# Six local-attention layers: cycles of half a sequence, one TensorE loop body, inverse roots by guess and products

## The reference, cut to what matters

```python
x = attn_layer(shift_tokens(x), Wqkv[i], ...) + x     # 16 heads of 64, window 32, look back one window
x = ffn_layer(shift_tokens(x), ln_g[i], ...) + x      # layer norm, 128 -> 2x341, gelu gate, -> 128
# in attn_layer, for q and k: t / max(norm(t), 1e-12) * scale, then the rotary turn with tables for every token
```

## Time and profile before

| | us |
|---|---|
| median of 3 runs (lowest, highest) | 4182.8 (4181.38, 4186.91) |
| the profiled execution's own time | 4189.23 |
| its span in the trace | 4187.4 |
| PE busy | 3726.9 (89%) |
| DVE busy | 3097.7 (74%) |
| POOL busy | 2984.4 (71%) |
| ACT busy | 2239.1 (53%) |

### The profile page before, as it was taken

How to read it: one execution, slowest core, us unless ns; L and a number is a source line. 1 busy time by engine, 2 the same in 40 slices (tenths; PEclk the granted TensorE clock), 3 DMA queues, 4 the chain that set the end, 5 groups by cost and what they waited for, 6 DMA issues and landing times. The chain is left out here.

```text
span 4187.4 us, 157873 instructions
## 1 busy us (share of the span) xinstructions
PE 3726.9 (89%) x67688; PEld 2899.3 (69%) x67880; DVE 3097.7 (74%) x4664; ACT 2239.1 (53%) x2808; POOL 2984.4 (71%) x1330
## 2 busy tenths in 40 slices
PE   6888886899999899999999999999899998999995
PEld 4555554677777677777777777777777777777773
DVE  3455454778788788887787877787878788887883
ACT  3444443556565565555555655565555555555551
POOL 1100103888888788888888888888878888888882
PEclk9999997999999999999999999999999999999997
DMA  1000000222222322222322223222223222222221
GB/s 50 4 5 3 3 5 21 70 78 67 63 63 70 80 64 64 64 69 59 81 68 64 59 68 84 64 64 64 69 55 84 64 67 59 69 64 64 64 64 51
DMA packets 162242, 239.53 MB, mean 57 GB/s; under 512 B 42258, under 2 KB 60632, under 8 KB 161496
## 3 DMA queue, kind: packets, MB, share of 16 engines
q1 hardware_dynamic: 161624, 230.00, 21.3%
HBM read 21.00 MB, written 4.19 MB: 6 GB/s over the span
## 5 line engine op out<-in xcount | busy, mean ns | idle before, releaser
L1057 POOL TENSOR_TENSOR norms<-floors,minus_half 128x16 f32<-128x16 f32 x384 | 1127.9, 2937 | 212.4 <-DVE floors L1397 212.3
L1061 POOL TENSOR_TENSOR by_cos<-by_cos,by_sin 128x1024 f32<-128x1024 f32 x384 | 947.0, 2466 | 268.9 <-DVE by_sin L1390 266.4
L1067 POOL TENSOR_TENSOR by_cos<-by_cos,norms 128x1024 f32<-128x1024 f32 x384 | 734.2, 1912 | 29.5
L1290 ACT ACTIVATE squares<-proj 128x1024 f32<-128x1024 f32 x384 | 393.3, 1024 | 491.9 <-PE proj L1132 453.5
L1388 DVE TENSOR_TENSOR by_cos<-proj,turns 128x1024 f32<-128x1024 f32 x384 | 468.9, 1221 | 246.7 <-ACT squares L1290 200.8
L1130 PE MATMUL proj<-qkv_hi,xs_hib 128*128 128x512 f32 x1152 | 537.3, 466 | 41.8 <-DVE by_sin L1390 26.9
L1394 DVE TENSOR_REDUCE sumsb<-squares 128x16 f32<-128x1024 f32 x384 | 464.7, 1210 | 89.8 <-ACT squares L1290 89.8
L1132 PE MATMUL proj<-qkv_hi,xs_lob 128*128 128x512 f32 x1152 | 468.4, 407 | 0.0
L1131 PE MATMUL proj<-qkv_lo,xs_hib 128*128 128x512 f32 x1152 | 467.7, 406 | 0.0
L1390 DVE TENSOR_TENSOR by_sin<-proj,turns 128x1024 f32<-128x1024 f32 x384 | 466.0, 1214 | 0.0
L1139 PE MATMUL ring<-ident,by_cos 128*128 128x128 f32 x3072 | 408.9, 276 | 6.8 <-issue 5.8
(11 more groups left out here) (171 smaller groups left out, 7397.2 us busy)
## 6 DMA issues: line engine op xcount, KB each, us to landing
v_win<-vb SPq DMA_DIRECT2D x1152, 130.0 KB
v_win<-vb SPq DMA_DIRECT2D x768, 65.0 KB
in_qkv<-L_ffn_Wqkv SPq DMA_DIRECT2D x12, 768.0 KB
wo<-L_ffn_Wo SPq DMA_DIRECT2D x6, 512.0 KB, 4.1
x_tok<-L_attn_x SPq DMA_DIRECT2D x8, 256.0 KB, 4.6
residual<-x_tok SPq DMA_DIRECT2D x8, 256.0 KB, 2.0
o_x<-residual SPq DMA_DIRECT2D x1, 2048.0 KB, 7.9
out<-o_x SPq DMA_DIRECT2D x8, 256.0 KB, 2.3
```

Source lines behind the costliest of these rows:

```text
L1057: nc.gpsimd.tensor_tensor(norms[:, t % 2, j, :], floors[:, t % 2, j, :], c["minus_half"][:, 0:H], ALU.pow).then_inc(e[f"{w_}_norm"].sem, 1)
L1061: nc.gpsimd.tensor_tensor(by_cos[:, j, :], by_cos[:, j, :], by_sin[:, j, :], ALU.add).then_inc(e[f"{w_}_added"].sem, 1)
L1067: nc.gpsimd.tensor_tensor(heads, heads, norms[:, t % 2, j, :].unsqueeze(2).broadcast_to([P, H, DH]), ALU.mult).then_inc(e[f"{w_}_ready"].s ...
```

## The change

- A cycle is now half a sequence (two tiles, `PER = 2`), and the feed-forward part runs once for each half in 256 columns, two halves later (`LAG = 2`). `Events` give more credit (`ahead`).
- PE has one loop body for every half of a layer. What differed between cycles is moved off PE: the mask of a sequence's first window is copied by a DMA into `mask_now` once for each half, the wait for `Wo` is on ACT, the bias product of a new layer stands ahead of the loop. The other engines keep loops over sequences 2 to 6 with two halves in the body and write out four halves around each layer's end.
- kT holds two tiles as a ring, EK waits for the scores of the tile before. `by_cos` is doubled. C waits for the transposes of two tiles before and for A of the tile before.
- The power on POOL for the norms is replaced: ACT makes a guess for q and k together (IG, an Exp of the floor's bits read as an integer), and POOL refines it with two Newton rounds of four products of 128 x 32, each waiting for the one before. The floor for q and k is one DVE instruction.
- DG is gone; spread is two transposes for each half of f_rstd broadcast over 128 columns.
- A layer's w1 is scaled inside the ACT copy and the DVE subtraction, and one DVE instruction (L1447) goes.

```diff
 CYCLE = {
+    "PE": "Tq:0 mean Pq:2 X:-1 O:-2 V:-1 Tk:0 Pk:2 var S:0 spread Tk:1 Pv:2 Tq:1 W:-2 O:-1 Pq:3 X:0 W:-1 V:0 "
+    "Pk:3 GG AA S:1 Pv:3 F4",
+    "Act": "XF XSa:2 EV:1 EXP:-1 EQ:0 Qq:2 EX:-1 IG:1 EO:-2 XSa:3 FSQ EK:0 Qk:2 XH EK:1 EV:2 EQ:1 EXP:0 IG:2 "
+    "EO:-1 Qq:3 EX:0 Qk:3 GEL",
+    "DVE": "XSd:2 Rk:1 XC Rq:2 Cq:2 R:-1 FV Ck:2 XM MX:0 SB:0 XSd:3 Rk:2 XL WX:-2 Cq:3 WX:-1 Rq:3 R:0 Ck:3 AM "
+    "MX:1 SB:1 XN",
+    "Pool": "Aq:0 N:0 Mq:0 Ak:0 Mk:0 Aq:1 Ak:1 N:1 Mk:1 FP Mq:1",
+    "SP": "VM:0 VM:1",
 }
...
+            def inverse_roots(t, when):
+                x, y, z = floors[:, t % 2, :], norms[:, t % 2, :], newton[:, :]
+                wait_tile(pool, "guess", t, when)
+                for n, limit in enumerate((c["three"], c["twelve"])):
+                    if n:
+                        wait_tile(pool, "newton", t, when, 4)
+                    nc.gpsimd.tensor_tensor(z, y, y, ALU.mult).then_inc(e["newton"].sem, 1)
+                    wait_tile(pool, "newton", t, when, 4 * n + 1)
+                    nc.gpsimd.tensor_tensor(z, z, x, ALU.mult).then_inc(e["newton"].sem, 1)
+                    wait_tile(pool, "newton", t, when, 4 * n + 2)
+                    nc.gpsimd.tensor_tensor(z, limit[:, :], z, ALU.subtract).then_inc(e["newton"].sem, 1)
+                    wait_tile(pool, "newton", t, when, 4 * n + 3)
+                    nc.gpsimd.tensor_tensor(y, y, z, ALU.mult).then_inc(e["newton" if n == 0 else "norm"].sem, 1)
...
-                    nc.gpsimd.tensor_tensor(norms[:, t % 2, j, :], floors[:, t % 2, j, :], c["minus_half"][:, 0:H],
-                                            ALU.pow).then_inc(e[f"{w_}_norm"].sem, 1)
...
+                elif kind == "IG":
+                    wait_tile(act, "floor", t, when)
+                    for x in "qk":
+                        wait_tile(act, f"{x}_ready", t - 2, when)
+                    nc.scalar.activation(norms[:, t % 2, :], floors[:, t % 2, :].bitcast(I32), ACT.Exp, scale=GUESS_SCALE,
+                                         bias=c["guess_bias"][:, 0:1]).then_inc(e["guess"].sem, 1)
...
                 elif kind == "spread":
-                    wait_seq(pe, "diag", cyc)
+                    wait_half(pe, "f_rstd", when)
-                    nc.tensor.matmul(out[:, 0:S], ones[:, :], diag[:, :, :].rearrange("p t n -> p (t n)"), start=True,
-                                     stop=True).then_inc(e["spread_full"].sem, 1)
+                    for i in range(PER):
+                        last = nc.tensor.transpose(out[:, i * P:(i + 1) * P], f_rstd[:, i:i + 1].broadcast_to([P, P]),
+                                                   ident[:, :])
+                    last.then_inc(e["spread_full"].sem, 1)
...
+            for at in range(-LEAD, LAG):
+                cycle(at, None, at)
...
+            with pe.Fori(0, DEPTH - 1) as layer:
+                bias_of(layer, pe.snap(layer * STEPS + LAG))
+                with nc.Fori(LAG, STEPS + LAG, engines=one, hint_back_edge=True) as n:
+                    cycle(pe.snap(layer * STEPS + n), layer)
```

More of the change, by code:

```diff
@@ L759 @@
 PART = {"q": 0, "k": 1, "v": 2}
-CYCLE = {
[10 rows of a table removed]
-}
[L774 to L779, removed]
+HALVES = S // (2 * P)
+PER = TILES // HALVES
+HS = PER * P
+STEPS = B * HALVES
+LEAD = 2
+BIAS_SLOT = 0
+GUESS_SCALE = float(-0.5 * np.log(2.0) / 2 ** 23)
+GUESS_BIAS = float(0.5 * np.log(2.0) * (127 - 0.043))
+GUESS_ERROR = 3.33e-4
+ROOT_SCALE = 16.0
+LAG = 2
+CYCLE = {
+    "PE": "Tq:0 mean Pq:2 X:-1 O:-2 V:-1 Tk:0 Pk:2 var S:0 spread Tk:1 Pv:2 Tq:1 W:-2 O:-1 Pq:3 X:0 W:-1 V:0 "
[6 more added lines that the diff above has]
+    "SP": "VM:0 VM:1",
+}
+FFN = ("XF", "mean", "XC", "FSQ", "var", "FV", "FP", "spread", "XM", "XH", "XL", "GG", "GEL", "AA", "AM", "F4", "XN")
+RELEASE = {"Tq": ("q_T", 1), "Tk": ("k_T", 1), "X": ("pT", 1), "V": ("attn", 2), "O": ("oT", 1), "W": ("x_mid", 1),
+           "mean": ("centred", 1), "var": ("f_var", 1), "spread": ("xn", 1), "GG": ("gelu", FC), "AA": ("gated", FC),
+           "F4": ("x_new", 1)}
+RINGS = ("Tq", "Tk", "X", "V", "O", "W", "mean", "var", "spread", "GG", "AA", "F4")
 def tokens(engine):
@@ L803, in in_cycle, with steps_of @@
 def in_cycle(name, t):
-    return next(at for _, n, at in tokens("PE") if n == name and (at - t) % TILES == 0)
-def steps_of(engine, kind):
+    return next(at for _, n, at in tokens("PE") if n == name and (at - t) % PER == 0)
+def steps_of(engine, at=None, begin=0, end=None):
     steps = []
-    for token, name, t in tokens(engine):
[L813 to L835, removed]
@@ L963, in run, with wait_tile @@
[L963 to L968, removed]
-            def middle(layer):
[L971 to L975, removed]
+        def wait_tile(eng, name, t, when, k=1):
+            base, p = when
+            eng.wait_ge(e[name].sem, e[name].at((t + PER * p) * (e[name].per // PER) + k, base))
@@ new lines, in wait_half, with wait_moved, where, columns @@
+        def wait_half(eng, name, when, k=1):
+            base, p = when
+            eng.wait_ge(e[name].sem, e[name].at((p - LAG) * e[name].per + k, base))
+        def wait_moved(eng, t, when):
+            base, p = when
+            moved = e[f"v_moved{t % PER}"]
+            eng.wait_ge(moved.sem, moved.at((p + t // PER) * 160 + 160, base))
+        def where(b, p, t):
+            off, tile = divmod(PER * p + t, TILES)
+            return (off % B if b is None else b + off), tile
+        def columns(b, p, t, rows, begin, end):
+            seq, tile = where(b, p, t)
+            return xT[rows, bass.ds(seq, 1), 1 + tile * P + begin:1 + tile * P + end].rearrange("p a n -> p (a n)")
@@ new lines, in layers_stage, with run, cycle @@
+        low, high, every = slice(0, P // 2), slice(P // 2, P), slice(0, P)
+        def run(eng, name, step, new_layer=lambda layer: None):
+            def cycle(when, b, layer, *place):
+                for s_, t, token, ahead in steps_of(name, *place):
+                    step(s_, t, token, when, b, layer + ahead if ahead else layer)
+            def middle(layer):
+                with eng.Fori(LAG, B - 1) as b:
+                    base = eng.snap(layer * STEPS + b * HALVES)
+                    for p in range(HALVES):
+                        cycle((base, p), b, layer)
+            for at in range(-LEAD, HALVES * LAG):
+                cycle((0, at), None, 0, at)
@@ L976, in run @@
             with eng.Fori(0, DEPTH - 1) as layer:
-                cycle("second", layer * B + 1, 1, layer)
                 new_layer(layer)
                 middle(layer)
-                cycle("last", layer * B + (B - 1), B - 1, layer + 1)
-                cycle("first", layer * B + B, 0, layer + 1)
-            cycle("second", (DEPTH - 1) * B + 1, 1, DEPTH - 1)
+                base = eng.snap(layer * STEPS)
+                for at in range(STEPS - HALVES, STEPS + HALVES * LAG):
+                    cycle((base, at), None, layer, at)
@@ L983, in run @@
             middle(DEPTH - 1)
-            cycle("end", DEPTH * B - 1, B - 1)
-            cycle("tail", DEPTH * B, 0)
+            for at in range(STEPS - HALVES, STEPS + HALVES * LAG):
+                cycle(((DEPTH - 1) * STEPS, at), None, DEPTH - 1, at, 0, PER * STEPS)
         def all_loaded(new):
             return new * (16 * LOADS) + 16 * LOADS
-        def previous(b):
-            return B - 1 if isinstance(b, int) and b == 0 else b - 1
-        def following(b):
-            return 0 if isinstance(b, int) and b == B - 1 else b + 1
@@ L1033, in _ @@
             sp.wait_ge(padded, 2)
-            run(sp, "SP", step, new_layer=new_layer)
+            run(sp, "SP", step, new_layer)
             sp.wait_ge(loaded, DEPTH * 16 * LOADS)
@@ L1181, in step @@
                 elif kind == "O":
-                    wait_tile(pe, "attn", t, cyc, 2)
-                    out = take(SLOT[token], cyc, "oT", tile_at("oT", t, 1), new)
+                    wait_tile(pe, "attn", t, when, 2)
+                    out = take(token, kind, t, when, new)
                     for i in range(PAIRS):
@@ new lines, in ffn @@
+                    wait_half(pe, "f_rstd", when)
+                    out = take(token, kind, t, when, new)
+                    for i in range(PER):
+                        last = nc.tensor.transpose(out[:, i * P:(i + 1) * P], f_rstd[:, i:i + 1].broadcast_to([P, P]),
+                                                   ident[:, :])
+                    last.then_inc(e["spread_full"].sem, 1)
+                elif kind in ("GG", "AA"):
+                    part, full = (1, "gate_full") if kind == "GG" else (0, "up_full")
+                    wait_half(pe, "xn_lo", when)
+                    out = take(token, kind, t, when, new)
+                    for k in range(FC):
+                        cols, at = slice(k * P, (k + 1) * P), slice(k * HS, (k + 1) * HS)
+                        nc.tensor.matmul(out[:, at], w1_hi[:, part, cols], xn_hi[:, :], start=True, stop=False)
```

(40 more changed lines are left out.)

506 lines of the change are left out of this document (247 added, 259 removed), and 10 rows, old and new, of the table CYCLE.

## The result

The changed kernel takes 4067.47 us (median of 4, 4064.95 to 4078.89) against 4184.85 for the kernel before in the same runs: ratio 0.9722, 95% interval 0.9699 to 0.9746. 3986 was forecast, in a range of 3890 to 4140; the sign was right, and the gain is 117 us where 197 were expected. The profiled execution took 4078.89 us with a span of 4077.1 and is the longest of the four.

A forecast was written before the change was run, and what follows sets the result against it. PE's own stream was taken to set the cycle. 693 + 108 + 94 x 32.6 (3064) + 55 (layer ends) + 38 + 32 = 3990 us of span, so a time of 3986 us; range 3890 to 4140.

The forecast's parts named there:

- The instruction stream: PE's loop body: some 1420 instructions stay on PE without fetches, so the 2.7 us of "issue" per sequence go.
- The half: Half a sequence on PE: takes 32.6 us, 65.2 for a sequence instead of 68.6; range 31.8 to 34.
- X's slot: Ring slot for PE's X: EQ frees it at 5.9 us, X starts at 6.0; loss 0 to 0.5 us a half, taken as 0.
- The wait ahead of V: PE at V:-1: waits 0.3 us a half for EX, which cannot begin before Qq:2 ends.
- POOL: POOL's norms: 0.22 us a product, 23.5 us busy a half; relief gives nothing beyond 1.1 us ahead of spread.
- Spread: PE's spread: the 1.1 us wait for POOL's diagonal goes, and transposes save 0.5 us, for each sequence.
- DVE and ACT: Busy times: DVE 27.0 us a half, 83% of 32.6; ACT 46.5 of 65.2 us a sequence.
- The stretches of L1373: DVE pieces slowed beside POOL products: each may lose 0 to 2.1 us; 0.2 us a half added.
- Layer ends: Cycles around a layer's end: 11 us extra an end instead of 18.3, 55 for five; bounds 5 and 20 an end.
- Filling: Start of the layers' stage, before the full halves: 108 us instead of 112.8.
- draining: End of the layers' stage, two partial halves and the last feed-forward chain: 38 us instead of 27.
- The first: Rival: the denser order waits more, through DVE and the ring; a half of 34.0 us, 4118 us in all; chance 0.2.

The follow-up runs named there:

- e4_body2: The changed kernel with two halves in PE's loop body (some 2840 instructions) and half as many passes: 4518.25 us, ratio to before 1.0813.
- e1_table: The changed kernel with one Exp of one column added on ACT ahead of EV:1, so the table load runs there: 3995.24 us, ratio to before 0.9558.
- e2_v4: The changed kernel with four value buffers in the place of two: 3992.34 us, ratio to before 0.9548.
- h1_pow: The changed kernel with the early one-column Exp, four value buffers, and POOL's power in place of guess and products: 4072.44 us, 88 over the same without the power.
- g5_spread: The kernel before with only POOL's diagonal removed and spread done by four transposes: 4203.78 us, ratio to before 1.0077.
- g7_nohint: The changed kernel without the back-edge hint on both of PE's loops: 4071.8 us, ratio to before 0.9747.
- e3_pow: The changed kernel with one power on POOL again in place of ACT's guess and the eight products: 4089.38 us, ratio to before 0.9788.

## Why the prediction was right and where it missed

- **The instruction stream: right.** The body of some 1420 instructions stays on PE; no fetch, no "issue". The changed kernel less this one thing (e4_body2) is 8% slower than before, so in this order the gain can't be had without it. The old order with a body that stays was not run, and neither were half cycles, the merged floor or the w1 scaling alone, so no run shares the 117 us out among the parts. The 2.7 us a sequence that I gave it was the size seen in the old order; in the new one the fetches cost 9.6 a sequence (451 / 47).
- **The half: 32.6 forecast, 33.6 measured; this term missed.** 94 x 33.6 is 94 us over my 3064, and the whole error is 4077.1 - 3990 = 87. In my walk X's slot was free at 5.9 us against X's start at 6.0, and I took the 0 of "0 to 0.5 us" there. That is the step that failed. The prediction has the table load ahead of EXP but no wait of EV for the window DMAs, and the load comes only behind EV, so both lie in one chain ahead of X, which waits 0.9 us a half. e1_table and e2_v4 each take 72 to 75 us back, at 32.4 to 32.7 a half: the 32.6 of the prediction is what the order gives without that chain.
- **The wait ahead of V** was in the walk with 0.3 us and is 0.6.
- **POOL: the price right** (0.24 to 0.28 us a product for 0.22; 21.7 us a half for 23.5), "nothing beyond the wait ahead of spread" roughly so here (22 us), wrong once the chain on ACT is gone (88 us in h1_pow).
- **Spread: wrong as a gain of its own.** The 1.1 us a sequence went into the sum as if nothing stood behind that wait. In the kernel before it came back ahead of X and GG (g5_spread); the changed kernel has no wait there, but its waits ahead of X and V are 1.5 us a half.
- **DVE and ACT:** 26.5 us a half for 27.0, 22.6 for 23.3. The stretches of L1373 that I priced at 0.2 us a half did not come (below).
- **Layer ends** 6.7 us for 11, but the 94 halves hold 3209.7 - 94 x 33.6 = 51 us over the plain sum, for 55: the rest, some 17, lies mostly at the start of the loop's second copy, for the last layer (halves of 39.5 and 38.0 us; six pieces of 16 KB on q8 from 3513 to 3548 us), and where it gives way to the straight code of the end (39.4 and 37.6 us; 14 pieces from 3934 to 4038). The prediction had no term for these two places. **Filling** 101.7 for 108, **draining** 41.6 for 38.
- **The rivals.** The first (a denser order that waits more) is what happened in part, and its 4118 us are nearer to the 4067 than my 3986 is. The sign that it named, waits of over 1 us a half ahead of X and V, came with 0.9 and 0.6, while the half is outside the 32 to 33 us that were to show the sum. It gave DVE and the ring as the reason; X's slot was in it, DVE was not what made PE wait.

## What to carry to other kernels

Count the instructions of a loop body on the engine that bounds, look in the queue of instructions whether a pass fetches, and cut the body until it doesn't; what the fetches cost depends on the order around them. Before a wait is priced as a gain, ask what the next instruction of the same engine would have waited for: here the wait for POOL's diagonal hid one for EXP, and ACT's chain hid what POOL's power costs. In an engine that runs in order, write down for each instruction every wait it has, buffers that DMAs still read included, and put a table load where the engine waits anyway.

## What the runs showed of the hardware

PE's loops of about 1100 instructions (the attention block's, one piece in 385 us) and 1420 (none from 900 to 3400 us) go round without a fetch, the second with or without the hint at the back edge (g7_nohint). One of 2840 fetches 370 pieces of 16 KB in 2400 us, about 12 a pass, and the kernel before with 2700 moves 376. The Trainium skill (Runtime: NRT & Kernel Launch, Instruction fetch mechanics) gives PE 2048 instructions. That lies between 1420 and 2700, and no run here narrows it further. For PE the runs speak against what the Trainium skill says in the same section, that a taken branch outside a window of two pages must fetch.

The power on POOL costs by the element: 2.94 us for 16 values, 5.52 for 32, 0.7 for 2 (L1113). Eight dependent products over 128 x 32 take 2.6 us.

The slow xs_lo of the kernel before (L1373, 64 x 256, 2.27 us as mean of 34 from 1000 to 3400 us) has no like in the changed kernel:

```profile
L1428 DVE TENSOR_TENSOR xs_lob<-xT,xs_hib 64x128 fp32r<-64x128 f32 x141 | 40.7, 289 | 1.9
```

The traces show what decides. These are two pieces of the kernel before, each with the instruction of POOL that ran beside it:

```profile
2089.81 3.17 POOL L1057 TENSOR_TENSOR norms<-floors,minus_half 128x16 f32<-128x16 f32 x1 [1.08 <-DVE floors L1397]
2090.22 0.42 DVE L1373 TENSOR_TENSOR xs_lob<-xT,xs_hib 64x255 fp32r<-64x255 f32 x1
2117.91 2.15 POOL L1067 TENSOR_TENSOR by_cos<-by_cos,norms 128x1024 f32<-128x1024 f32 x1
2118.30 2.03 DVE L1373 TENSOR_TENSOR xs_lob<-xT,xs_hib 64x256 fp32r<-64x256 f32 x1
```

Beside the power a piece takes 0.42 us. Beside a sum or product of 1024 columns it ends 0.28 us after POOL's instruction does; so do all 51 slow pieces from 1000 to 3400 us. The 17 that began ahead of POOL's product took 0.41 us. In the changed kernel POOL is idle beside 275 of the 282 pieces, and none is slow. It isn't the lighter load of POOL: with the power back (e3_pow, h1_pow, where POOL is busy for 28.6 of some 33.5 us) 61 pieces of 128 columns in each run meet the end of POOL's sum, take up to 0.58 us instead of 0.28 and end 0.15 us behind it, and none waits longer. So it is where the pieces lie in time beside POOL's sums and products.
